# Last tiles of a relational graph layer: projections between product parts, x and bias added on TensorE, tiles centred one by one

## What is computed

```python
rel_ids = jnp.arange(1, weight.shape[0] + 1)
masks = (relation[None] == rel_ids[:, None, None, None]).astype(x.dtype)
h = jnp.einsum('rbnm,bmd->rbnd', masks, x)          # B 8, N 1024, D 128, R 4
y = jnp.einsum('rbnd,rdo->bno', h, weight) + bias
t = x + y
out = (t - mean(t)) / sqrt(var(t) + 1e-5)           # over the last axis
```

## Time and profile before

| | |
|---|---|
| median of 3 runs | 139.79 us (139.66 to 139.83) |
| the profiled execution | 138.68 us, of which the span of its instructions is 136.9 us |
| PE busy | 124.1 us (91%) |
| DVE / ACT / GpSimd busy | 85.8 / 83.0 / 69.2 us |
| chain that ended last | PE 73%, DMA 15%, SP's queue 4% |
| granted TensorE clock, mean | 0.985 |

### The profile page before, as it was taken

One profiled execution on the slowest core, in us unless ns is written; L12 is line 12 of the kernel. 1 busy time (PEld: TensorE's weight loads), 2 busy tenths in 40 slices (PEclk: granted clock), 3 DMA queues, 4 the chain that ended last, 5 costly groups with the idle time before them and its releaser, 6 DMA issues.

```text
span 136.9 us, 2235 instructions
## 1 busy us (share of the span) xinstructions
PE 124.1 (91%) x727; PEld 77.2 (56%) x727; DVE 85.8 (63%) x270; ACT 83.0 (61%) x85; POOL 69.2 (51%) x79
## 2 busy tenths in 40 slices
PE   5986799489999999999999999999999999997920
PEld 2355688346564747465565656565656474666810
DVE  1185213765758494958677675757585939488851
ACT  3655753379785848484848586777758484513040
POOL 3000019975295709680786259553957195405440
PEclk9999999999999999999999999999999999999985
DMA  4999969999999999999999999999913000300422
GB/s 125 415 427 418 427 230 419 421 426 414 426 426 406 423 421 421 420 423 417 412 419 424 414 424 424 424 412 414 382 59 158 0 0 0 153 0 0 160 77 84
DMA packets 7789, 42.24 MB, mean 309 GB/s; under 512 B 864, under 2 KB 1376, under 8 KB 3936
## 3 DMA queue, kind: packets, MB, share of 16 engines
q1 hardware_dynamic: 7776, 42.08, 75.3%
HBM read 37.88 MB, written 4.19 MB: 307 GB/s over the span
## 4 chain that ended last, share of the span: by engine, by line
PE 73%; DMA 15%; SPq 4%; ACT 2%; DVE 1%; issue 1%; POOL 1%
PE h_ps L194 54%; DMA adj_sb<-in_adj_dram 15%; PE y_ps L201 10%; PE tp_ps L178 9%; ACT mask L171 1%; SPq L152 1%; SPq L258 1%; SPq L155 1%; POOL scale L219 1%; ACT h_sb L392 0%; DVE out_sb L223 0%; DVE stats L207 0%; ACT out_sb L398 0%; SPq L270 0%; SPq L269 0%
## 5 line engine op out<-in xcount | busy, mean ns | idle before, releaser
L171 ACT ACTIVATE mask<-adj_sb 128x2048 fp8e4<-128x2048 int32 x30 | 57.2, 1906 | 9.0 <-DMA adj_sb<-in_adj_dram 9.0
L194 PE MATMUL h_ps<-maskT,x_sb 128*128 128x512 fp8e4 (+1 forms) x152 | 32.0, 352 | 3.5 <-DVE maskT L182 2.5
L194 PE MATMUL h_ps<-maskT,x_fine 128*128 128x512 fp8e4 (+1 forms) x152 | 32.0, 352 | 0.4 <-DVE x_fine L164 0.4
L194 PE MATMUL h_ps<-maskT,x_rest 128*128 128x512 fp8e4 (+1 forms) x152 | 32.0, 352 | 0.1
L182 DVE COPY maskT<-tp_ps 128x512 uint32<-128x512 uint32 x30 | 20.6, 686 | 17.2 <-PE tp_ps L178 17.2
L167 POOL TENSOR_TENSOR x_bias<-x_sb,bias_sb 128x1024 f32<-128x1024 f32 x8 | 19.0, 2380 | 18.2 <-DMA bias_sb<-in_L_gnn_bias_dram 18.2
L194 PEld LDWEIGHTS h_ps<-maskT,x_sb 128*128 128x128 bf16 x152 | 14.3, 96 | 18.7 <-DVE maskT L182 2.9
L335 POOL TENSOR_SCALAR minus_mean<-mean_var 128x4 f32<-128x4 f32 (+1 forms) x16 | 3.1, 193 | 41.7 <-issue 22.9
L477 DVE TENSOR_TENSOR total<-y_ps,x_bias 128x512 f32<-128x512 f32 (+1 forms) x17 | 11.2, 660 | 20.2 <-issue 19.2
L386 ACT COPY h_sb<-h_ps 128x512 f32<-128x512 f32 x13 | 7.6, 585 | 23.4 <-issue 23.4
L178 PE MATMUL tp_ps<-identity,mask 128*128 128x128 f32 x128 | 21.1, 286 | 0.7 <-ACT mask L171 0.4
(11 more groups left out here) (28 smaller groups left out, 46.4 us busy)
## 6 DMA issues: line engine op xcount, KB each, us to landing
adj_sb<-in_adj_dram SPq DMA_DIRECT2D x30, 1024.0 KB, 17.6
x_sb<-in_x_dram SPq DMA_DIRECT2D x8, 512.0 KB, 17.9
out_dram<-out_sb SPq DMA_DIRECT2D x7, 512.0 KB, 7.7
adj_sb<-in_adj_dram SPq DMA_DIRECT2D x4, 512.0 KB, 5.2
out_dram<-out_sb SPq DMA_DIRECT2D x1, 256.0 KB, 2.0
out_dram<-out_sb SPq DMA_DIRECT2D x2, 128.0 KB, 1.8
bias_sb<-in_L_gnn_bias_dram SPq DMA_DIRECT2D x1, 64.0 KB, 14.8
w_sb<-in_L_gnn_weight_dram SPq DMA_DIRECT2D x1, 64.0 KB, 14.6
```

What stands on the lines that cost most here:

```text
L171: nc.scalar.activation(mask[:, slot % NMASK], adj_sb[:, slot % NADJ], ACT.Copy, saturate=False).then_inc(done, 1)
L194: last = nc.tensor.matmul(h_ps[:, bank, 0:n], x_t, m_t, start=(part == 0 and t == 0), stop=(part == PARTS - 1 and t == TILES - 1))
```

## The change

On PE, the parts of the two last quarters are issued one at a time (`quarter_part`), with `project_half(14)` after the first part of quarter (15, 0) and `project_quarter(15, 0)` after the first part of quarter (15, 1). The last quarter's `y` goes to two places, one per tile (`last_y`: a slice of `y_ps` and one of a `tp_ps` bank). There PE first multiplies `x_bias` by the identity, then adds the projection of the tile. ACT copies the last quarter's products tile by tile, and copies the first quarter's ahead of its `finish_half(13)`. DVE runs `find_others` ahead of `measure_half(13)`. For the last quarter it takes bn_stats from PSUM directly, aggregates, lifts the variance, and writes y - mean of both tiles to `total` after it has released GpSimd's power; then tile 4, then tile 6 times its scale. ACT does tile 7 times its scale. SP waits for one more `act_normed` before the last store.

```diff
@@ -238,6 +242,9 @@
                 eng.wait_ge(by_chunk, u - PIECED + 1)
             else:
                 eng.wait_ge(by_piece, O * (u + 1))
+
+        def last_y(o):
+            return y_ps[:, 0, 0, :] if o == 0 else tp_ps[:, 1, 0:D]
 
         block = ctx.enter_context(nc.Block())
 
@@ -281,7 +288,7 @@
             store(sp, LAST, LAST, HALF[0], stored)
             for c in range(2):
                 sp.wait_ge(normed, CH * LAST + 3 + c)
-                sp.wait_ge(act_normed, CH * LAST + 3)
+                sp.wait_ge(act_normed, CH * LAST + 3 + c)
                 store(sp, LAST, LAST, QUARTER[2 + c], stored)
 
             sp.wait_ge(flag_ready, 1)
@@ -419,17 +426,26 @@
             convert(7)
             finish_half(0)
             convert(8)
-            for hf in range(2, HALVES - 1):
+            for hf in range(2, HALVES - 2):
                 copy_half(hf)
                 if 2 * hf + 5 < UNITS:
                     convert(2 * hf + 5)
                 finish_half(hf - 1)
                 if 2 * hf + 6 < UNITS:
                     convert(2 * hf + 6)
+            copy_half(HALVES - 2)
             copy_quarter(HALVES - 1, 0)
-            copy_quarter(HALVES - 1, 1)
+            finish_half(HALVES - 3)
+            act.wait_ge(multiplied, 2 * HALVES)
+            for o in range(O):
+                nc.scalar.copy(h_sb[:, (HALVES - 1) % 2, O + o], h_ps[:, bank_of(HALVES - 1, 1), o * P:(o + 1) * P]
+                               ).then_inc(tile_copied, 1)
             finish_half(HALVES - 2)
             finish(LAST, (HT + 1,), 2 * (HALVES - 1) + 1, 1)
+            act.wait_ge(scaled, 2 * HALVES)
+            act.wait_ge(centred, 2)
+            nc.scalar.activation(out_sb[:, LAST, TILES - 1, :], total[:, LAST % NTOTAL, TILES - 1, :], ACT.Identity,
+                                 scale=scale[:, LAST % 2, TILES - 1:TILES]).then_inc(act_normed, 1)
 
             act.wait_ge(flag_ready, 1)
             again = act.value_load(flag[0:1, 0:1], min_val=0, max_val=P)
@@ -538,21 +554,33 @@
                 if hf >= 1:
                     add_half(hf - 1)
                 empty_bank(2 * hf + 3)
+                if hf == HALVES - 2:
+                    find_others()
                 if hf >= 1:
                     measure_half(hf - 1)
                 if hf >= 2:
                     finish_half(hf - 2)
-            find_others()
             finish_half(HALVES - 3)
             add_half(HALVES - 2)
             measure_half(HALVES - 2)
             add_quarter(0)
             measure_quarter(0)
             finish_half(HALVES - 2)
-            add_quarter(1)
-            measure_quarter(1)
+            for o in range(O):
+                dve.wait_ge(tile_projected, o + 1)
+                nc.vector.bn_stats(stats[:, LAST % 2, TILES - O + o, :], last_y(o)).then_inc(tile_measured, 1)
+            dve.wait_ge(tile_measured, O)
+            aggregate_rows(LAST % 2, QUARTER[CH - 1], aggregated, 1)
+            dve.wait_ge(aggregated, 2 * HALVES)
+            lift_variance(LAST % 2, QUARTER[CH - 1], var_ready, 1)
+            for o in (1, 0):
+                nc.vector.tensor_scalar(total[:, LAST % NTOTAL, TILES - O + o, :], last_y(o),
+                                        mean_var[:, LAST % 2, TILES - O + o, 0:1], None, ALU.subtract).then_inc(centred, 1)
             finish_quarter(0, (HT,))
-            finish_quarter(1, (HT + O, HT + O + 1))
+            dve.wait_ge(scaled, 2 * HALVES)
+            dve.wait_ge(centred, 2)
+            nc.vector.tensor_scalar(out_sb[:, LAST, TILES - O, :], total[:, LAST % NTOTAL, TILES - O, :],
+                                    scale[:, LAST % 2, TILES - O:TILES - O + 1], None, ALU.mult).then_inc(normed, 1)
             dve.wait_ge(flag_counted, 1)
             nc.vector.tensor_copy(flag[:, :], tp_ps[0:1, 0, 0:1]).then_inc(flag_ready, 1)
 
@@ -633,15 +661,20 @@
                         turn(2 * hf + 3)
                 last.then_inc(multiplied, 2)
 
-            def products_quarter(hf, c):
+            def quarter_part(hf, c, part):
                 b = hf // 2
                 place = (2 * hf + c) % NMT
-                wait_chunk(pe, piece_evacuated, evacuated, 2 * hf + c)
+                if part == 0:
+                    wait_chunk(pe, piece_evacuated, evacuated, 2 * hf + c)
+                if hf % 2 == 0 and c == 0:
+                    x_ready(part, b)
+                last = part_products(part, b % NX, b % 2, slice(place, place + 1), bank_of(hf, c))
+                if part == PARTS - 1:
+                    last.then_inc(multiplied, 1)
+
+            def products_quarter(hf, c):
                 for part in range(PARTS):
-                    if hf % 2 == 0 and c == 0:
-                        x_ready(part, b)
-                    last = part_products(part, b % NX, b % 2, slice(place, place + 1), bank_of(hf, c))
-                last.then_inc(multiplied, 1)
+                    quarter_part(hf, c, part)
 
             def keep_warm(times):
                 for _ in range(times):
@@ -675,13 +708,24 @@
             turn(5)
             for hf in range(2, HALVES - 1):
                 products_half(hf)
-            products_quarter(HALVES - 1, 0)
+            quarter_part(HALVES - 1, 0, 0)
             project_half(HALVES - 2)
+            quarter_part(HALVES - 1, 0, 1)
+            quarter_part(HALVES - 1, 0, 2)
+            quarter_part(HALVES - 1, 1, 0)
             project_quarter(HALVES - 1, 0)
-            products_quarter(HALVES - 1, 1)
+            quarter_part(HALVES - 1, 1, 1)
+            quarter_part(HALVES - 1, 1, 2)
             pe.wait_ge(flag_step, 3)
             nc.tensor.matmul(tp_ps[0:1, 0, 0:1], above[:, 1:2], ones[:, 0:1], start=True, stop=True).then_inc(flag_counted, 1)
-            project_quarter(HALVES - 1, 1)
+            pe.wait_ge(biased, B)
+            pe.wait_ge(added, 2 * (HALVES - 1))
+            for o in range(O):
+                nc.tensor.matmul(last_y(o), identity[:, :], x_bias[:, LAST % 2, TILES - O + o, :], start=True, stop=False)
+            for o in range(O):
+                pe.wait_ge(tile_copied, o + 1)
+                nc.tensor.matmul(last_y(o), h_sb[:, (HALVES - 1) % 2, O + o], w_sb[:, 0, :], start=False,
+                                 stop=True).then_inc(tile_projected, 1)
 
             pe.wait_ge(flag_ready, 1)
             again = pe.value_load(flag[0:1, 0:1], min_val=0, max_val=P)
```

More of the change, by code:

```diff
@@ L117, in relational_layer @@
         act_normed = sem("act_normed")
+        tile_copied = sem("tile_copied")
+        tile_projected = sem("tile_projected")
+        tile_measured = sem("tile_measured")
+        centred = sem("centred")
         stored = sem("stored")
```

## The result

The changed kernel takes 137.94 us (median of 22 runs, 137.14 to 139.03) against 139.27 us for the kernel before (22 runs, 138.23 to 139.99): a ratio of 0.9918, 95% interval 0.9889 to 0.9947. The profiled execution took 137.59 us.

What follows compares the result with a forecast made beforehand. DVE's queue was taken to bound the tail, with PE and ACT 1.1 us early. Gains of 0.6 and 0.12 us less 0.07 for stores gave 0.65 us off 139.79: 139.15 us, range 138.55 to 139.8.

Steps and rivals of the forecast that it cites:

- What bounds the kernel: In the tail, DVE's queue, delayed by find_others' new place, starts the last quarter's bn_stats at 131.2 us, not 131.80.
- The size of the sum: In the tail: statistics 0.6 us earlier plus 0.12 us at the end, less 0.07 for stores: 0.65 us off.
- The base: The median of 139.79 us, 1.11 us above the profiled execution, from which the 0.65 us was taken unchanged: 139.15 us.
- The stores: Last two stores, 0.45 us apart instead of 1.2: sharing the DMA engines costs 0 to 0.2 us, taken as 0.07.
- Rival A: In the tail PE, not DVE, sets the end: bn_stats at 129.9 us, gain 1.95 us, 137.85 us; chance 0.08.
- Rival B: At the last power, GpSimd's port holds DVE's tile 4 to its end: 0.53 us off, 139.25 us; chance 0.12.
- Rival C: GpSimd's powers of halves 13, 14 and last quarter stretched 0.32 us each by DVE: 0.31 us slower, 140.1; chance 0.08.
- D: Last stores collide in full (0.2 us) and the last power is partly stretched: 0.25 us off, 139.55 us; chance 0.12.

## Why the prediction was right or wrong

- **What bounds the kernel: right.** DVE's queue, not PE, sets the start of the last quarter's statistics, because find_others moved out of the wait for GpSimd. The steps are there nearly as counted: DVE's finish_half(13) at 126.16 (forecast 126.3), add_half(14) at 126.71 (126.9), y at 130.05 and 130.27 (129.9 and 130.1), bn_stats at 130.95 (131.2), half 13's power 1.07 us (1.08). DVE's lag behind the first of the two y was 0.90 us; the forecast's own times, 129.9 and 131.2, gave 1.3.
- **The size of the sum: the mis-sized terms.** Against the start of the tail bn_stats came 0.18 us earlier than counted: the scales of half 13 were there 0.05 us sooner, the two normalizations of finish_half(13) and of finish_half(14) hold DVE for 0.55 us each and not 0.6, and 0.03 us are rounding in between. ACT's last tile took 0.40 us, not the 0.48 of the earlier trace rows; it is the one scaling on ACT without a bias operand; DVE's took 0.29. These 0.08 us and 0.01 of the last power make it 0.27 us. With 0.07 us of an earlier start, 0.65 becomes the 1.0 us by which the spans differ.
- **The base: the step that put the time outside the range.** I took 139.79 us, the median of three runs, as the level to subtract from, and noted 1.11 us between it and the profiled execution without asking where they lie. They are the distance between the two groups: all three runs were of the upper one, and the profiled execution of the lower. So "carry a difference over to the median unchanged" failed: a median over both groups moves with their shares. Of the 1.21 us between 139.15 and 137.94, 0.35 are the terms above (the upper group of the changed kernel lies at 138.80, inside the range), and 0.86 are the step from there to the median of 22 executions, 14 of them in the lower group. Against the profiled execution (138.68) my own sum gave 138.03; the measured one is 137.59. The range was built only from costs in the tail and held nothing for the base. Its lower end is also mis-added: 139.15 less the 0.07 and a third of 1.3 us is 138.65, not 138.55; that changes nothing here.
- **The stores: right.** From the last tile's end to the span's end it is 2.7 us both before and after, so less than 0.1 us was given back (forecast 0.07); landing took 1.9 in place of 1.8 us.
- **Rival A** (PE sets the end) gave 137.85 us, 0.1 from the measured median, but that is chance: DVE had no idle time ahead of bn_stats, and the nearness comes from the base. A is what the changed kernel becomes with find_others back, and that is worth 0.82 us, not 1.3, since y was only 0.90 us ahead of bn_stats.
- **Rival B** fell. Tile 4's normalization started at 132.34, inside the last power (132.00 to 132.72), and took its 0.34 us. The Trainium skill ("SBUF — State Buffer", Who interferes with whom) would have it blocked to the power's end, if it runs in a 2-port mode, which no trace shows; no run here shows VectorE held. The other direction does show: half 13's power took 1.40 or 1.41 us in each kernel with find_others beside it and 1.07 in each with find_others ahead.
- **Rival C** fell: the powers took 1.07, 1.01 and 0.72 us. **D** fell: the stores gave back less than 0.1 us and the last power was 0.72 us as before.
- **What I overlooked:** with the old order on ACT, find_others early costs 2.2 us of span, as its own run shows. The changed kernel escapes that only because the copy moved ahead of finish_half(13). That move alone gives 1.08 us of tail, and the rest of the change, find_others' new place included, adds nothing to it.

## What to carry to other kernels

Work that fills an engine's wait is free only where the wait is: before moving it, list what is queued behind the wait it filled, on that engine and on every engine that gets its input from there. When a matrix engine waits for a copy, look first at what the copy is queued behind; one line on ACT gave here what a new order on PE was meant to give. And when the runs that are known lie together but a microsecond away from the profiled execution, ask for the cause before taking their median as the level to subtract from.

The fastest version by its median is the changed kernel with find_others in its old place: 136.73 us against 138.69 us, ratio 0.9842 (0.979 to 0.9895). Its four executions were all of the lower group; against the lower group of the kernel before (near 138.6) that is 1.9 us. With the flag matmul last the tail is 0.15 us shorter still, and the two executions of the lower group took 136.6 us.

## What the runs showed of the hardware

- A wait of 1.86 us on PE was followed, during the next products, by some 3 us at 0.50 of the clock; the kernel before has a wait of 0.81 us at the same place and keeps 1.00. The same was seen in three profiles after PE's waits near 25 to 27 us (1.73 and 1.97 us; 1.33 and 0.79 in the third), and not in others with waits of 1.72 to 1.81 us; the two groups of executions lie 1.15 us apart.
- ACT's scaling took 0.40 us for 128x128 with a scale operand alone and 0.48 to 0.49 with scale and bias; DVE's tensor_scalar took 0.29 us with one operand and 0.34 with two, and from PSUM 0.34 with one and 0.41 with two.
- bn_stats of one tile from PSUM took 0.27 to 0.30 us; from SBUF the 64 of the kernel before took 0.28 us on average.
